# Routing weights of a mixture of experts: broadcast transfers in fp32 in place of a picking matmul

## The reference, cut to what matters

```python
scores = sigmoid(xf @ gate_weight.T)                       # 2048 x 32
...                                                        # bias, 4 of 8 groups, top 6
tw = take_along_axis(scores, topk_idx, axis=1)
tw = tw / (tw.sum(-1, keepdims=True) + 1e-20)
combine = zeros((T, E)).at[arange(T)[:, None], topk_idx].add(tw * 2.5)
def expert_step(acc, inp):
    gu, dn, c = inp                                        # c: the expert's weight per token
    g = xf @ gu[:64].T
    u = xf @ gu[64:].T
    return acc + c[:, None] * (silu(g) * u @ dn.T)
out = sum over the 32 experts + shared expert
```

## Time and profile before

| | us |
|---|---|
| three runs, median | 2182.18 |
| lowest, highest | 2181.0, 2187.54 |
| the profiled execution: time | 2176.0 |
| the profiled execution: span | 2174.2 |
| PE busy in the span | 1928.3 (89%) |
| DVE busy | 1422.8 (65%) |
| ACT busy | 1293.1 (59%) |
| POOL busy | 209.6 (10%) |
| mean granted PE clock | 0.95 |

### The profile page before, as it was taken

The page is one execution under the profiler, slowest core; times in us unless marked ns, Lnnn a source line. Parts: engine busy times, 40 slices in busy tenths (PEclk is TensorE's granted clock), DMA queues, the critical chain, the costliest instruction groups (busy, mean ns, idle before and its releaser), DMA issues. The chain is left out here.

```text
span 2174.2 us, 62632 instructions
## 1 busy us (share of the span) xinstructions
PE 1928.3 (89%) x27120; PEld 1183.2 (54%) x27120; DVE 1422.8 (65%) x2440; ACT 1293.1 (59%) x1831; POOL 209.6 (10%) x183
## 2 busy tenths in 40 slices
PE   8899999999897676998699999999999996767888
PEld 5577777777644443333355665665655653344332
DVE  3677777767536755554578888888888874475444
ACT  3477777777633752222277787787787775375222
POOL 4000000000201601111000000000000000050000
PEclk9899999999999788999799999999999998878999
DMA  3455454554202100111645445445445530210100
GB/s 139 121 129 140 124 133 132 130 135 123 42 0 32 28 5 22 42 36 54 105 78 93 85 93 93 85 93 93 86 92 93 86 62 2 31 31 6 39 24 29
DMA packets 63917, 161.44 MB, mean 74 GB/s; under 512 B 21796, under 2 KB 26020, under 8 KB 63268
## 3 DMA queue, kind: packets, MB, share of 16 engines
q1 hardware_dynamic: 61828, 154.33, 33.1%
q10 hardware_dynamic: 1824, 3.20, 0.7%
HBM read 68.13 MB, written 1.05 MB: 32 GB/s over the span
## 5 line engine op out<-in xcount | busy, mean ns | idle before, releaser
L594 ACT ACTIVATE Pb<-ps 128x1024 f32<-128x1024 f32 (+2 forms) x640 | 634.2, 1002 | 207.3 <-PE ps L543 159.5
L648 DVE TENSOR_REDUCE MX<-ps 128x2 f32<-128x804 f32 (+1 forms) x386 | 368.6, 985 | 61.4 <-PE ps L510 60.2
L563 PE MATMUL ps<-Pb,V 128*17 128x64 f32 (+1 forms) x13312 | 360.1, 248 | 9.9 <-issue 5.0
L650 DVE TENSOR_REDUCE MX<-ps 128x1 f32<-128x402 f32 (+1 forms) x512 | 277.9, 570 | 101.5 <-PE ps L514 92.5
L563 PEld LDWEIGHTS ps<-Pb,V 128*17 128x17 f32 (+1 forms) x13312 | 256.2, 97 | 97.0 <-issue 64.5
L510 PE MATMUL ps<-KST,QW 50*128 50x402 bf16 (+1 forms) x1024 | 177.0, 341 | 24.7 <-ACT V L613 17.3
L543 PE MATMUL ps<-QW,KST 50*128 50x128 bf16 (+1 forms) x3328 | 166.0, 220 | 29.7 <-ACT Pb L594 29.3
L494 PE MATMUL ps<-W,CT 128*128 128x128 f32 (+1 forms) x1144 | 170.6, 289 | 0.0
L486 PE MATMUL ps<-CT,W 128*128 128x402 f32 (+1 forms) x352 | 147.6, 545 | 18.0 <-DMA CT<-ctxT 12.1
L543 PEld LDWEIGHTS ps<-QW,KST 50*128 50x128 bf16 (+1 forms) x3328 | 101.4, 96 | 113.5 <-ACT Pb L594 84.4
L514 PE MATMUL ps<-KST,QW 96*128 96x402 bf16 (+1 forms) x512 | 154.1, 339 | 3.9 <-issue 1.5
(11 more groups left out here) (239 smaller groups left out, 2744.6 us busy)
## 6 DMA issues: line engine op xcount, KB each, us to landing
CT<-ctxT SPq DMA_DIRECT2D x44, 800.5 KB, 4.8
KST<-HL SPq DMA_DIRECT2D x320, 100.1 KB, 3.0
KST<-C SPq DMA_DIRECT2D x320, 100.1 KB, 3.0
ABO<-ctxT SPq DMA_DIRECT2D x10, 800.5 KB, 5.4
T<-ctxT SPq DMA_DIRECT2D x10, 800.5 KB, 4.4
KST<-HL SPq DMA_DIRECT2D x128, 50.0 KB, 2.7
KST<-C SPq DMA_DIRECT2D x128, 50.0 KB, 2.7
CT<-experts SPq DMA_DIRECT2D x32, 192.0 KB, 2.3
```

The source lines that it names most:

```text
L563: mm = nc.tensor.matmul(ps[32 * quad:32 * quad + m, SUM, oc:oc + nh * S], V[0:n, b % 2, tile, v0:v0 + m], Pb[0:n, buffer(b, x), ti * att.W ...
L594: nc.scalar.activation(Pb[0:n, buffer(b, x), 0:banks * 512].rearrange("p (a c) -> p a c", a=banks), score_banks(b, x)[0:n, 0:banks, :], AC ...
L648: nc.vector.reduce_max(MX[:, b % 2, 2 * j:2 * j + 2], work(job)[:, :, 0:n], AX.X).then_inc(freed["dve"], 1)
L650: nc.vector.reduce_max(MX[:, b % 2, j:j + 1], work(job)[:, 0:n], AX.X).then_inc(freed["dve"], 1)
```

## The change

The weights are no longer split. `TW` is turned by 16 fp32 matmuls with the identity into four banks (6, 7, 0, 1), and ACT copies each bank into `BYE`, 32 rows of `C`: one row of 2048 fp32 weights for each expert. For each item SP issues two transfers, one for each expert: its row of 1024 tokens is read 64 times and written to the 64 partitions of that expert in one of two buffers `RW` (`Pb[:, 2:4]`). DVE's second product reads that buffer in place of PSUM. The pick matmul, the `picks` transfers and the bf16 parts are gone.

```diff
-            CBS = area(NT * E).bitcast(BF16).rearrange("p (t e) -> p t e", t=NT)
-            CTT = HL[0:2 * E, 0, :]
+            BYE = C[0:E, :]
+            RW = Pb[:, 2:4, :]
...
+            turned_banks = (6, 7, 0, 1)
...
-                link(nc.vector.tensor_scalar(TW, TW, ROUTE_SCALE, None, ALU.mult))
-                link(nc.vector.tensor_copy(CBS[:, :, 0:E], TW))
-                nc.vector.tensor_tensor(CBS[:, :, E:2 * E], TW, CBS[:, :, 0:E], ALU.subtract).then_inc(s["parts"], 1)
+                nc.vector.tensor_scalar(TW, TW, ROUTE_SCALE, None, ALU.mult).then_inc(s["parts"], 1)
             if role == "act":
-                eng.wait_ge(s["turned"], 1)
-                for i in range(2):
-                    nc.scalar.activation(CTT[:, i * 1024:(i + 1) * 1024], ps[0:2 * E, 6 + i, :].bitcast(BF16), ACT.Copy
-                                         ).then_inc(s["weights"], 1)
+                for i, bank in enumerate(turned_banks):
+                    eng.wait_ge(s["turned"], i + 1)
+                    nc.scalar.activation(ck(BYE, i), ps[0:E, bank, :], ACT.Copy).then_inc(s["weights"], 1)
...
-                    eng.wait_ge(s["weights"], 2)
                     eng.wait_ge(s["xlo"], NC)
...
-                    mm = nc.tensor.matmul(ps[:, 6 + cc, :], HL[0:2 * E, 1, slot * 128:(slot + 1) * 128],
-                                          ck(CTT, 2 * sweep + cc), start=True, stop=True)
...
             def down(sweep, item, slot, cc, last=False):
...
+                if slot is None and not sweep:
+                    eng.wait_ge(s["weights"], NC)
...
                     if not shared:
                         ins.then_inc(s["mid"], 1)
+                        if cc == 0:
+                            eng.wait_ge(spreads[buffer], (sweep * (NI - 1) + item - 1 - buffer) * 16 + 32)
                         eng.wait_ge(s["mid"], unit(sweep, item, cc) + 1 - 2 * (sweep + 1))
-                        ins = nc.vector.tensor_tensor(h, h, ps[:, 6 + cc, :], ALU.mult)
+                        ins = nc.vector.tensor_tensor(h, h, RW[:, buffer, cc * CH:(cc + 1) * CH], ALU.mult)
...
-                eng.dma_start(HL[0:2 * E, 1, slot * 128:(slot + 1) * 128], picks[item - 1]).then_inc(loads[slot], 16)
+            def sp_weights(sweep, item):
+
+                buffer = (item - 1) % 2
+                if item > 2:
+                    eng.wait_ge(s["hid"], unit(sweep, item - 2, 1) + 1)
+                elif sweep:
+                    eng.wait_ge(s["hid"], unit(0, NI - 2 + item - 1, 1) + 1)
+                for k in range(2):
+                    e = 2 * (item - 1) + k
+                    eng.dma_start(RW[64 * k:64 * k + 64, buffer, :],
+                                  BYE[e:e + 1, sweep * 1024:(sweep + 1) * 1024].unsqueeze(1).broadcast_to([1, 64, 1024])
+                                  ).then_inc(spreads[buffer], 16)
...
-                        for t in range(NT):
-                            tr = nc.tensor.transpose(ps[0:2 * E, 6 + t // 8, :].bitcast(BF16)[:, t % 8 * 128:(t % 8 + 1) * 128],
-                                                     CBS[:, t, :], wb("ident16"))
-                        tr.then_inc(s["turned"], 1)
+                        for i, bank in enumerate(turned_banks):
+                            for t in range(4):
+                                tr = nc.tensor.matmul(ps[0:E, bank, t * 128:(t + 1) * 128], TW[:, 4 * i + t, :], w("ident"),
+                                                      start=True, stop=True)
+                            tr.then_inc(s["turned"], 1)
...
+                    for item in range(1, SLOTS + 1):
+                        sp_experts(sweep, item)
+                    if not sweep:
+                        eng.wait_ge(s["weights"], NC)
+                    for item in range(1, NI):
+                        sp_weights(sweep, item)
+                        if item > 2 and item + 2 < NI:
+                            sp_experts(sweep, item + 2)
```

More of the change, by code:

```diff
@@ L1398, in moe_stage @@
                 link(nc.vector.tensor_tensor(TW, TW, SM.unsqueeze(2).broadcast_to([128, NT, E]), ALU.mult))
-                link(nc.vector.tensor_scalar(TW, TW, ROUTE_SCALE, None, ALU.mult))
-                link(nc.vector.tensor_copy(CBS[:, :, 0:E], TW))
-                nc.vector.tensor_tensor(CBS[:, :, E:2 * E], TW, CBS[:, :, 0:E], ALU.subtract).then_inc(s["parts"], 1)
+                nc.vector.tensor_scalar(TW, TW, ROUTE_SCALE, None, ALU.mult).then_inc(s["parts"], 1)
             if role == "act":
-                eng.wait_ge(s["turned"], 1)
-                for i in range(2):
-                    nc.scalar.activation(CTT[:, i * 1024:(i + 1) * 1024], ps[0:2 * E, 6 + i, :].bitcast(BF16), ACT.Copy
-                                         ).then_inc(s["weights"], 1)
+                for i, bank in enumerate(turned_banks):
+                    eng.wait_ge(s["turned"], i + 1)
+                    nc.scalar.activation(ck(BYE, i), ps[0:E, bank, :], ACT.Copy).then_inc(s["weights"], 1)
             NI = E // 2 + 1
             loads = [sem(f"moe_load{i}") for i in range(SLOTS)]
+            spreads = [sem(f"moe_weights{i}") for i in range(2)]
             def ew(item_slot, k):
@@ L1422, in up @@
                 if cc == 0 and slot is not None:
-                    eng.wait_ge(loads[slot], (sweep * (NI - 1) * 32 // SLOTS) + ((item - 1 - slot) * (32 // SLOTS)) + 32)
+                    eng.wait_ge(loads[slot], (sweep * (NI - 1) * 16 // SLOTS) + ((item - 1 - slot) * (16 // SLOTS)) + 16)
                 if sweep or not (isinstance(item, int) and item == 0):
@@ L1437, in up @@
                         for i, (a, b) in enumerate(((0, 0), (1, 0), (0, 1))):
-                            nc.tensor.matmul(ps[:, 2 + 2 * k + cc, :], WP[:, slot, a, k * D:(k + 1) * D],
-                                             ck(XP[:, b, :], 2 * sweep + cc), start=(i == 0), stop=(i == 2))
-                    mm = nc.tensor.matmul(ps[:, 6 + cc, :], HL[0:2 * E, 1, slot * 128:(slot + 1) * 128],
-                                          ck(CTT, 2 * sweep + cc), start=True, stop=True)
+                            mm = nc.tensor.matmul(ps[:, 2 + 2 * k + cc, :], WP[:, slot, a, k * D:(k + 1) * D],
+                                                  ck(XP[:, b, :], 2 * sweep + cc), start=(i == 0), stop=(i == 2))
                 mm.then_inc(s["gu"], 1)
@@ L1479, in act_item, with dve_item @@
                                          ).then_inc(s["gate"], 1)
-            def dve_item(sweep, item, shared=False):
+            def dve_item(sweep, item, shared=False, buffer=None):
                 for cc in range(2):
@@ L1489, in dve_item, with sp_experts @@
                         ins.then_inc(s["mid"], 1)
+                        if cc == 0:
+                            eng.wait_ge(spreads[buffer], (sweep * (NI - 1) + item - 1 - buffer) * 16 + 32)
                         eng.wait_ge(s["mid"], unit(sweep, item, cc) + 1 - 2 * (sweep + 1))
-                        ins = nc.vector.tensor_tensor(h, h, ps[:, 6 + cc, :], ALU.mult)
+                        ins = nc.vector.tensor_tensor(h, h, RW[:, buffer, cc * CH:(cc + 1) * CH], ALU.mult)
                     ins.then_inc(s["hid"], 1)
[L1494 to L1498, removed]
+            def sp_experts(sweep, item):
+                slot = (item - 1) % SLOTS
+                if sweep or item > SLOTS:
+                    eng.wait_ge(s["down"], unit(sweep, item, 0) - 2 * SLOTS + (2 if item > SLOTS else 0))
                 eng.dma_start(CT[:, slot // 2, slot % 2 * 3 * D:(slot % 2 + 1) * 3 * D], experts[item - 1]
                               ).then_inc(loads[slot], 16)
-                eng.dma_start(HL[0:2 * E, 1, slot * 128:(slot + 1) * 128], picks[item - 1]).then_inc(loads[slot], 16)
+            def sp_weights(sweep, item):
[9 more added lines that the diff above has]
+                                  ).then_inc(spreads[buffer], 16)
             if role == "sp":
@@ L1543, in moe_stage @@
                     with eng.Fori(0, NI // 2) as i:
-                        dve_item(sweep, i * 2 + 1)
-                        dve_item(sweep, i * 2 + 2)
+                        dve_item(sweep, i * 2 + 1, buffer=0)
+                        dve_item(sweep, i * 2 + 2, buffer=1)
                     for cc in range(2):
@@ L1561, in tree_stage @@
             loads = [sem(f"moe_load{i}") for i in range(SLOTS)]
-            loads_before = 2 * (E // 2) // SLOTS * 32
+            loads_before = 2 * (E // 2) // SLOTS * 16
             WOFF = (0, INNER, NODES, NODES + D, NODES + 2 * D)
```

## The result

The changed kernel takes 2603.44 us (median of four runs, 2593.76 to 2614.28), the kernel before 2182.01 us in the same series: a ratio of 1.195, 95% interval 1.1916 to 1.1984. The forecast was 2657 us with a range of 2590 to 2780 us. It is slower by 421 us, as forecast in kind; in size the forecast of 475 us was 54 us too much.

A forecast was written before the change was run, and what follows sets the result against it. TensorE bounds the kernel before, one-partition broadcasts after, at 20.2 us an item. Start, two sweeps of 303 us and the turn, less 1.3 us at the end, add 475 us: forecast 2657 us, range 2590 to 2780.

The forecast's parts named there:

- What bounds the kernel: Routed-expert stage before the change: TensorE sets the pace, 2.67 us a unit, 5.34 us an item; transfers are hidden.
- The broadcasts: Two one-partition transfers of 262 KB per item at 26 GB/s: 10.1 us each, 20.2 us an item.
- Does it hide?: Expert stage: no; transfers run without a break, the compute engines wait, and TensorE's 20.5 us saved are worth nothing.
- The expert rows: Expert loads of 192 KB, queued behind the broadcasts: under 1 us of engine time, wanted two items later, nothing added.
- The start and the turn: First pair lands at 866.8 us after 7.8 us of fp32 turning; between sweeps, item 16's products at 1169.9, next 1195.2.
- The end: End of the expert stage: 1.3 us shorter, since the last unit no longer waits for TensorE.
- The picks: Pick matmul leaves each of 64 units: 0.32 us each, 20.5 us saved if nothing else becomes late.
- Rival A: Broadcast row served at full rate, 3.3 us an item and hidden; unit 2.35 us, total 2165 us; chance 0.07.
- B: Broadcasts go like the mask copies, 12 GB/s from one partition: 43.7 us an item, about 3410 us; chance 0.04.
- C (one engine): A single DMA engine carries each broadcast: same 20.2 us an item, DMA share near 0.06; chance 0.85 together with forecast.
- D: Something between, such as neighbouring items' rows overlapping: 40 to 60 GB/s, 9 to 13 us an item, 2300 to 2430 us; chance 0.04.

The follow-up runs named there:

- experiment 2: Changed kernel, each transfer reading four source partitions 16 times each: neighbours 2685.17 us, 4 apart 2194.91 us, 32 apart 2362.15 us.
- experiment 5: Changed kernel with the second transfer of each item reading partition 64 + e, so its two rows lie 64 partitions apart: 2486.42 us.
- experiment 3: Changed kernel without any broadcast and without VectorE's wait for them, all else of the change kept: 2151.26 us.
- experiments 1: Changed kernel with each of the 64 destination partitions reading a row of its own partition instead of one row 64 times: 2151.34 us.
- experiment 6: Changed kernel with the weights by expert first written to HBM and broadcast from there: 2151.37 us, ratio 0.9866.
- experiment 4: Kernel before the change, its pick matmul taking all 128 rows with zeros in rows 64 to 127: 2167.28 us, ratio 0.9937.

## Why the prediction was right

*What bounds the kernel.* Right: TensorE before, the transfers after.

*The broadcasts.* Right in kind: the limit is at the source, one partition gives about what one engine moves, and it took the 8 KB copy out of one partition to see it. The term was mis-sized: "I take 26 GB/s", "an item 20.2 us"; it is 28.3 GB/s and 18.51 us. Over the 30 steps from item to item in the two sweeps this is 51 us, where the whole sum of 475 was 50 us too high; the other differences cancel. Of the 51, 28 us are the rate out of one group (27.2 GB/s, 19.26 us an item), and 22 us the shorter mean beside it, which the sum had put at nothing. The Trainium skill's 27.2 GB/s a port ("SBUF — State Buffer", section on Door 1 and the DMA port swizzle) is what the trace gives where one group alone is read, 128 packets in 19.26 us. One support of the 26 was luck: that "27 is what one engine moved at the best" says nothing of a partition, for some 15 of the 16 engines were busy at it (DMA share 0.95), and in experiment 2 four engines moved 92 GB/s out of four partitions 4 apart. The two rates happen to lie close together. What I could not say from the trace of before, whether the limit is by partition or by group, experiment 2 shows: four neighbours share one way out.

*Does it hide?* Right: the transfers run with hardly a break (DMA share 0.95), and TensorE's saving is worth nothing.

*The expert rows.* "Nothing added" holds for the time, but not for the reason given. They do stand behind the broadcasts, the issue of one takes 8.8 us in the rows above, and ScalarE waits 296.5 us for them; it costs nothing because the item waits for its broadcast as long, and the three steps of a sweep without a load ahead of their pair are no shorter than the rest (experiment 5).

*The start and the turn.* Start +14.8 us for 16.6 forecast: the fp32 turning took 6.2 us and not 7.8, and the pair landed 21.5 us after the first issue (21.6 forecast). Turn 26.9 us for 25.3: the first broadcast of sweep 1 was issued at 1157.35, 4.9 us after item 16's product began and not 3.7. The end was not shorter (1.3 us forecast).

*The picks.* "The pick leaves each unit: 64 x 0.32 = 20.5 us" was mis-sized, unseen in the result since the gain is hidden: experiment 3 gives 0.52 us a unit, 33 us. The start to the next start was the wrong measure, for the pick also delayed its neighbours. Rival A's time of 2165 us should have been 2151.

*Rivals.* A, a broadcast too short to matter, happens with a source of 64 partitions or in HBM: experiments 1 and 6. B is out, one partition gives 27 and not 12 GB/s; the mask copies were slow for another cause, which was not tried. C (one engine) is out by the DMA share near 1. D, an overlap between rows on different ways, is real (experiment 5). Here both rows of an item leave by the same way, and only every second step between items changes it; the 0.75 us an item by which the mean lies under 19.26 us are probably this, far from D's 9 to 13 us an item.

## What to carry to other kernels

Before a row is broadcast by DMA within SBUF, count the ways out on which the source lies, not the bytes or the destinations: four neighbouring partitions are one, and 0, 32, 64 and 96 were only two. Here each gave 25 to 28 GB/s, and a broadcast out of one took some 9 us of the transfers' time for 262 KB that went out of HBM in 3.9, latency included. A DMA share near 1 with a low GB/s is the sign: 40 GB/s over 16 engines at 0.96 is 2.6 GB/s for a busy engine, where the load of the earlier trace rows had 26. A matmul's price is the change in the period of its loop, not its own duration: one with 64 rows between ones with 128 cost 0.30 us more than the same with 128 rows.

## What the runs showed of the hardware that I had not expected

- A port read by all 16 engines gave 27.2 GB/s (128 packets of 4096 B in 19.26 us), one read by four engines 25 (21.1 us an item).
- Two ports read in turn through one queue gave nearly twice that (steps of 8.0 to 9.5 us) where no expert load stood between the pairs, and 14.9 to 17.2 us a step where one did (experiment 5).
- Zeros in place of missing rows make the pick faster (experiment 4): 0.22 us and not 0.32 to the next start, and 0.10 us less on both neighbours.
- Slow transfers hold the issuing engine: SyncE's issue of one broadcast took up to 9.6 us and 5.1 in the median, where the same broadcast out of HBM took 0.60 in the median (experiment 6) and an expert load before 0.34. What stands behind them in the queue waits too: an expert load landed 21.7 us after its issue, 2.3 before.

```profile
L1510 SPq DMA_DIRECT2D Pb<-C x64: 469/5076/9631, 853.2 to 1425.4; - x64
```
